# Causal attention stages of a decoder: probabilities made in their turned form from a second score product

## The chip, the cores and the metric

The program runs on one NeuronCore of a Trainium2 chip. The metric is the device time of one execution in microseconds, median of several. A core has five engines with queues of their own that meet only by semaphores: TensorE (PE: matmuls, and PEld: its weight loads), VectorE (DVE), ScalarE (ACT), GpSimd (POOL) and SyncE (SP, which issues DMAs).

## The reference, cut to what matters

Four decoder layers, each of three sub-blocks, on x of 16 items x 128 positions x 256 channels. Two of the sub-blocks hold causal self-attention over 16 heads of 16 channels: the first half of `_L1_ffn_ref` (layer norm ahead, no query, key or value bias) and `_L3_attn_ref` (with biases). Both are

```python
q = (x @ wq).reshape(b, t, HEADS, HEAD_DIM)          # keys and values likewise
scores = jnp.einsum('bqhd,bkhd->bhqk', q, k)
mask = jnp.arange(t)[:, None] < jnp.arange(t)[None, :]
scores = jnp.where(mask, -jnp.inf, scores)
attn = jax.nn.softmax(scores / np.sqrt(HEAD_DIM), axis=-1)
ctx = jnp.einsum('bhqk,bkhd->bqhd', attn, v).reshape(b, t, EMB)
return ctx @ wo + bo
```

## The kernel before, in words

The program is a row of stages, one for each sub-block, which keep x on the chip. `build` (L3823) makes them; `first_causal` (L3849) and `causal` (L3870) are `self_attention_stage` (L395) with `causal=True`. Each engine runs its part of a stage in the written order, and semaphore counts (`Count`, L34) tie them. A stage goes over 16 batch items. An item is split into two units (u = 0, 1; `NP` = 2) of eight heads, and the eight into two banks i of four heads k. In what follows n is a unit's number, 2b+u.

For one unit TensorE writes the causal mask into the two banks of `s_ps[u]` (two bf16 products with 512 columns, L643) and adds eight score products, queries in the rows (L650). A product has 32 contraction rows, so it occupies one of four row groups of the array: unit u uses groups 2u and 2u+1. There are two pairs of score banks, one for each unit of an item. VectorE takes the negated row maximum over all eight heads (L879). ScalarE makes `probs` by eight exponentials with the maximum as bias, each with a sum (L798). VectorE inverts the sums (L919), GpSimd multiplies (L569), TensorE turns the scaled probabilities by four transposes per bank (L664), ScalarE copies bank 0 and VectorE bank 1 to `pT` (L806, L886), and TensorE multiplies by the values (L690: four column groups of 32, one head pair in each). VectorE copies the context to `aT` (L912), TensorE multiplies by `wo` (L701), VectorE adds the residual (L926, or L929 with norm and moments).

Projections for the next item are laid between: queries and keys (L612, L620) in units u = 0, values (L629) in u = 1. `bank_d` is shared by keys, values and the output product, so that the value projection waits for the residual addition. ScalarE takes the queries from PSUM (L771, or L775 with biases), VectorE the keys and values (L893 to L906). GpSimd fetches x for item b+2 (L516, with norm L519 to L526), and adds the output bias (L549).

On TensorE the order of a unit is written out by hand in `unit` (L708): half of the transposes of the previous unit, projections, the weighing of the unit before that, the other half, the next unit's scores, the output product. Middle items run in a loop (`every_item`, L474).

A stage's beginning: GpSimd makes the constants (L500) and fetches two items; TensorE waits for weights and constants (L746) and turns item 0 (L605). The second stage begins inside the experts' stage ahead of it (`begun=True`): that stage issues its weight loads (L2361) between its own gathers, calls its constants and its fetches on GpSimd (L2443, L2450), and `take_first` and `take_second` on ScalarE (L2611).

Of the kernel before, what the change touches and what calls it, by code (L numbers as in the profile page):

```python
# [15 lines left out]
ALU = mybir.AluOpType  # L16
ACT = mybir.ActivationFunctionType
AX = mybir.AxisListType
F32 = mybir.dt.float32
BF16 = mybir.dt.bfloat16  # L20
# [3 lines left out]
P = 128  # L24
B = 16
# [83 lines left out]
def chunked(w, rows=P):  # L109

    return w.rearrange("(c p) n -> p c n", p=rows)


def row_everywhere(v, parts=P):

    return v.rearrange("(o n) -> o n", o=1).broadcast_to([parts, v.shape[0]])
# [272 lines left out]
def half_scales():  # L389

    low = (np.arange(P) // HEAD_DIM) % 2 == 0
    return (np.stack([low, ~low], axis=1) * np.float32(HEAD_DIM ** -0.5)).astype(np.float32)


def self_attention_stage(core, halves, wq, wk, wv, wo, out_bias, qkv_bias=None, causal=False, alibi=False,  # L395
# [10 lines left out]
    with ExitStack() as ctx:  # L406
# [595 lines left out]
        if context is not None:  # L1002
            c_used.advance(B)
            for n in c_landed:
                n.advance(16 * B)
        stage = Stage(sync, gpsimd, tensor, scalar, vector, out_used, x_saved if norm else out_used)
        stage.start = Start(load_weights, constants, fetch_two, take_first, take_second, biases, tables)
# [2815 lines left out]
def build(nc, a, out):  # L3823
    with ExitStack() as ctx:
# [18 lines left out]
        with ExitStack() as moe:  # L3843
# [4 lines left out]
            core.side = "right"  # L3848
            first_causal = self_attention_stage(core, a["half_scales"], a["L1_ffn_wq"], a["L1_ffn_wk"], a["L1_ffn_wv"],  # L3849
                                                a["L1_ffn_wo"], a["L1_ffn_bo"], causal=True, target=x1, norm=False,  # L3850
                                                pre_norm=(a["L1_ffn_ln1_scale"], a["L1_ffn_ln1_shift"]), after=over_context)
            core.side = "left"
# [16 lines left out]
        core.side = "left"  # L3869
        causal = self_attention_stage(core, a["half_scales"], a["L3_attn_Wq"], a["L3_attn_Wk"], a["L3_attn_Wv"],  # L3870
                                      a["L3_attn_Wo"], a["L3_attn_bo"], causal=True,
                                      qkv_bias=(a["L3_attn_bq"], a["L3_attn_bk"], a["L3_attn_bv"]), after=experts_b, begun=True)
        experts_b.leads_to(causal)
# [40 lines left out]
def laid_out(inputs):  # L3914
# [22 lines left out]
    a["head_rows"] = wide_head_rows()  # L3937
    a["half_scales"] = half_scales()
    a["mask_cols"] = a["mask_BxS2_fk1"].T
    a["lens_cols"] = a.pop("mask_BxS2_if0").T  # L3940
# [27 lines left out]
```

## Time and profile before

| | us |
|---|---|
| median of 3 runs (lowest, highest) | 3044.0 (3043.15, 3044.74) |
| profiled execution | 3048.76 |
| its span, first to last instruction | 3047.0 |

| engine | busy share of the span |
|---|---|
| PE, PEld | 88%, 73% |
| DVE | 53% |
| ACT | 46% |
| POOL | 46% |

The mean granted TensorE clock is 0.94 of full speed. Times of rows are us from the span's start. A busy PE means that some matmul is in flight; matmuls overlap, and a row's duration holds the last one's own flight. In a row that stands for several instructions (x4) the duration runs from the first start to the last end. The first causal stage lies at about 1124 to 1330, the second at about 2544 to 2742.

### The profile page before, as it was taken

How to read it: one execution, taken by the hardware profiler on the slowest of the kernel's cores; microseconds unless marked ns; L12 is line 12 of the kernel's file. 1: busy time of each engine (PE TensorE's matmuls, PEld its weight loads, DVE VectorE, ACT ScalarE, POOL GpSimd, SP SyncE). 2: the span in 40 equal slices, each digit the busy share in tenths (PEclk: the TensorE clock that was granted, in tenths of full speed). 3: DMA queues.
4: the chain of work that ended last, by engine and by line, in shares of the span. 5: the costliest groups of instructions: out<-in, count | busy, mean ns of one | idle time of the engine just before them, and what ended most of it. 6: DMA issues, size and time to landing. Idle time of an engine off the chain costs nothing.

```text
span 3047.0 us, 73166 instructions
## 1 busy us (share of the span) xinstructions
PE 2693.3 (88%) x26131; PEld 2215.5 (73%) x26189; DVE 1605.5 (53%) x3526; ACT 1412.8 (46%) x4543; POOL 1409.6 (46%) x1645
## 2 busy tenths in 40 slices
PE   7888897569989978978995889999996996999999
PEld 6777776447666656758994767878775995768888
DVE  7999999654456645561126763333333004556643
ACT  4666665434456647742226862223322335763210
POOL 3777777723356655543335662323232223663320
PEclk9999999769999989979997989999996998999999
DMA  3000000100000000027752020000005551010100
GB/s 100 2 2 2 2 2 2 56 30 1 24 15 14 17 20 1 0 84 237 240 195 77 0 95 8 11 10 7 10 19 178 180 171 53 0 49 29 53 10 20
DMA packets 96096, 154.49 MB, mean 51 GB/s; under 512 B 12256, under 2 KB 55904, under 8 KB 95600
## 3 DMA queue, kind: packets, MB, share of 16 engines
q1 hardware_dynamic: 89904, 134.92, 13.5%
q0 software_dynamic: 5952, 16.26, 1.5%
q8 instruction: 163, 2.67, 0.4%
q14 instruction: 77, 0.63, 0.1%
HBM read 136.74 MB, written 14.42 MB: 50 GB/s over the span
## 4 chain that ended last, share of the span: by engine, by line
PE 55%; POOL 4%; DVE 4%; issue 3%; ACT 3%; DMA 1%; SPq 0%; DVEq 0%; ACTq 0%; POOLq 0%
PE up_ps L2485 7%; PE e_out_ps L2503 5%; PE t_ps L664 4%; PE s_ps L650 3%; PE bank_a L1554 3%; PE bank_b L1554 3%; POOL probs L569 2%; PE bank_a L612 2%; PE bank_d L701 2%; ACT probs L798 2%; PE frame_ps L1633 2%; PE bank_d L620 2%; PE bank_b L1570 2%; PE bank_a L1570 2%; PE o_ps L690 2%
## 5 line engine op out<-in xcount | busy, mean ns | idle before, releaser
L569 POOL TENSOR_TENSOR probs<-probs,inv 128x512 f32<-128x512 f32 x320 | 327.9, 1039 | 277.8 <-DVE inv L919 277.5
L3437 POOL TENSOR_TENSOR hc<-h,bc 128x1024 f32<-128x1024 f32 x128 | 301.9, 2359 | 111.9 <-DVE h L3718 85.8
L798 ACT ACTIVATE probs<-s_ps,negmax 128x128 f32<-128x128 f32 (+1 forms) x768 | 297.1, 414 | 7.5 <-DVE negmax L879 6.0
L3718 DVE TENSOR_TENSOR_SCAN h<-da,dbu_ps 128x1024 f32<-128x1024 f32 x128 | 292.5, 2285 | 11.2 <-DVE dbu_ps L3730 4.6
L664 PE MATMUL t_ps<-ident,probs 128*128 128x128 f32 x1280 | 210.6, 288 | 57.7 <-POOL probs L569 49.5
L2485 PE MATMUL up_ps<-xT,w_lift 128*128 128x128 f32 x1984 | 234.3, 277 | 0.0
L664 PEld LDWEIGHTS t_ps<-ident,probs 128*128 128x128 f32 x1280 | 140.7, 142 | 124.9 <-POOL probs L569 58.4
L2485 PEld LDWEIGHTS up_ps<-xT,w_lift 128*128 128x128 f32 x1984 | 229.4, 194 | 0.1
L3665 ACT ACTIVATE da<-dta_ps 128x1016 f32<-128x1016 f32 x128 | 130.3, 1018 | 148.6 <-PE dta_ps L3527 148.3
L3527 PE MATMUL dta_ps<-dt,a_spread 32*128 32x128 f32 x2048 | 151.9, 287 | 44.6 <-ACT da L3665 20.8
L879 DVE TENSOR_REDUCE negmax<-s_ps 128x4 f32<-128x1024 f32 (+1 forms) x128 | 156.6, 1223 | 46.5 <-PE s_ps L650 44.5
L3527 PEld LDWEIGHTS dta_ps<-dt,a_spread 32*128 32x128 f32 x2048 | 127.5, 190 | 68.4 <-ACT da L3665 30.5
L806 ACT ACTIVATE pT<-t_ps 128x512 f32<-128x512 f32 x160 | 95.6, 597 | 164.7 <-PE t_ps L664 163.3
L2410 POOL DMA_INDIRECT rows<-expert_rows_in,row_from x62 | 60.3, 973 | 233.7 <-PE x_ps L2478 216.6
L798 ACT ACTIVATION_READ_ACCUMULATOR probs<-s_ps,negmax 128x1 f32 x768 | 168.3, 219 | 0.0
L3730 DVE TENSOR_TENSOR dbu_ps<-dbu_ps,bc 128x1024 f32<-128x1024 f32 x128 | 154.9, 1210 | 11.6 <-PE dbu_ps L3532 11.5
L2503 PE MATMUL e_out_ps<-w_down,hT 128*128 x680 | 156.7, 380 | 0.0
L3532 PE MATMUL dbu_ps<-dtu,spread 32*128 32x128 f32 x2048 | 152.0, 288 | 1.2 <-DVE h L3718 1.2
L1708 ACT ACTIVATE probs<-s_ps,negmax 128x128 f32<-128x128 f32 x256 | 89.9, 377 | 111.5 <-DVE negmax L1774 111.5
L2503 PEld LDWEIGHTS e_out_ps<-w_down,hT 128*128 128x128 f32 x680 | 124.8, 191 | 14.3
L650 PE MATMUL s_ps<-kT,q_low 32*128 32x128 f32 (+1 forms) x1024 | 130.6, 331 | 0.0
L3532 PEld LDWEIGHTS dbu_ps<-dtu,spread 32*128 32x128 f32 x2048 | 127.0, 190 | 1.5 <-DVE h L3718 1.5
(503 smaller groups left out, 6552.5 us busy)
## 6 DMA issues: line engine op xcount, KB each, us to landing
w_lift<-in_L_ffn_w SPq DMA_DIRECT2D x78, 512.0 KB, 4.7
w_lift<-in_L_ffn_w SPq DMA_DIRECT2D x23, 1024.0 KB, 5.0
cT<-in_ctx_turned SPq DMA_DIRECT2D x32, 256.0 KB, 2.6
w_down<-in_L_ffn_w SPq DMA_DIRECT2D x8, 1024.0 KB, 9.4
gathered<-expert_rows_out SPq DMA_DIRECT2D x12, 512.0 KB, 6.5
c_in<-in_ctx SPq DMA_DIRECT2D x16, 256.0 KB, 2.8
w_down<-in_L_ffn_w SPq DMA_DIRECT2D x8, 512.0 KB, 5.9
wkv<-in_L_xattn_Wkv SPq DMA_DIRECT2D x2, 2048.0 KB, 13.0
```

What stands on the lines that cost most here:

```text
L569: pool.tensor_tensor(probs[:, u % 2, i], probs[:, u % 2, i], inv[:, u % 2, HB * i:HB * (i + 1)].unsqueeze(2).broadcast_to([P, HB, W]), ALU ...
L650: last = pe.matmul(s_bank[:, i, k * W:(k + 1) * W], q[s][row:row + ROWS, j, qc, :], kT[row:row + ROWS, j, qc, :], start=not causal, stop=True,
L664: last = pe.transpose(t_ps[:, k * kt + t, :], probs[:, u % 2, i, k, t * P:(t + 1) * P], core.ident[:, :])
L798: last = act.activation(probs[:, u % 2, i, k, :], src, ACT.Exp, bias=negmax[:, u % 2, at], accum_out=sums[:, u % 2, at])
L879: dve.tensor_reduce(negmax[:, u % 2, :], scores, AX.X, ALU.max, negate=True).then_inc(negmax_done.sem, 1)
L1554: last = pe.matmul(bank[:, m, :], w[:, cc, col:col + P], src[:, cc, :], start=(cc == 0), stop=(cc == chunks_in - 1))
L2485: last = pe.matmul(up_ps[:, bank, m, :], lift_sb[:, i % LIFTS, k, cc, at:at + P], xT[:, i % 2, cc, :], start=(cc == 0), stop=(cc == DC - 1))
L2503: last = pe.matmul(out_ps[i % 2][:, 0:D], hT[:, i % 2, m, :], down_sb[:, e, m, :], start=(m == 0), stop=(m == HC - 1))
L3437: pool.tensor_tensor(hc[:, s % 4], h[:, s % 2], bc[:, j, 1, :].unsqueeze(1).broadcast_to([P, 2 * G, P]), ALU.mult).then_inc(hc_ready.sem, 1)
L3527: last_a = pe.matmul(dta_ps[:, i, g, :], a_spread[row:row + ROWS, s // 2, g, :], dt[row:row + ROWS, j, s // 2, :], start=True, stop=True)
L3532: last_u = pe.matmul(dbu_ps[si % 2][:, i, g, :], spread_sb[row:row + ROWS, g, :], dtu[row:row + ROWS, ji, si // 2, :], start=True, stop=True)
L3718: dve.tensor_tensor_scan(flat(h[:, s % 2]), flat(da[:, s % 4]), dbu_ps[s % 2][:, :, :, :].rearrange("p i g t -> p (i g t)"), 0.0, ALU.mult ...
```

## The change

Both causal stages move to a new function, `turned_attention_stage`. Scores are computed twice: queries in the rows, for the maximum alone, and keys in the rows, into `t_ps`, from which the exponential gives `pT` directly. For the second form the maximum must be subtracted per column: VectorE splits the negated maximum into three bf16 terms (`row_max`), TensorE turns the terms (`turn_max`), ScalarE copies them (`take_max`), and for each head a small product with a 0/1 matrix (`lower`) puts the sum of the terms into the bank ahead of the turned score. The mask is written ahead of the plain scores only; GpSimd zeroes later keys in `pT` (`leave_later_keys`). Sums come from products with ones (`counted`) beside the values, and VectorE divides the context (`take_context`). There is one pair of score banks and one pair of turned banks. The loops are written out. Constants grow from three to eight, and there is one more small weight load (`max_heads`).

```diff
+            def leave_later_keys(n):
+                pool.wait_ge(exp_done.sem, exp_done.done(n))
+                flat = pT[:, n % 2].rearrange("p i k t -> p (i k) t")
+                pool.affine_select(out=flat, in_=flat, compare_op=ALU.is_ge, fill=0.0, base=0,
+                                   pattern=[[0, 8], [1, P]], channel_multiplier=-1).then_inc(causal_done.sem, 1)
...
+            pool.wait_ge(loads.sem, weights)
+            pool.tensor_copy(which_max[:, :, :], heads_sb[:, :].unsqueeze(2).broadcast_to([P, 4, P])
+                             ).then_inc(consts.sem, 1)
...
+            def project_v(b):
+                pe.wait_ge(k_ready.sem, k_ready.done(b))
+                pe.wait_ge(out_used.sem, out_used.done(b - 2))
...
+            def leave_out(n):
+                pe.wait_ge(negmax_done.sem, negmax_done.done(n - 1))
...
+            def lower(n, i, k):
+                row = ROWS * (2 * (n % 2) + i)
+                pe.matmul(t_ps[:, i, k, :], which_max[row:row + ROWS, k, :], negmax_T[row:row + ROWS, :],
+                          start=True, stop=False, skip_group_check=True)
+
+            def score_both(n):
+                if n >= 0:
+                    pe.wait_ge(max_ready.sem, max_ready.done(n))
+                    pe.wait_ge(exp_done.sem, exp_done.done(n - 1))
+                    for k in range(4):
+                        for i in range(2):
+                            lower(n, i, k)
+                if n + 1 < UNITS and (n + 1) % 2 == 0:
+                    pe.wait_ge(q_ready.sem, q_ready.done((n + 1) // 2))
+                    pe.wait_ge(k_ready.sem, k_ready.done((n + 1) // 2))
+                for k in range(4):
+                    for i in range(2 if n + 1 < UNITS else 0):
+                        plain_last = score(n + 1, i, k)
+                    for i in range(2 if n >= 0 else 0):
+                        turned_last = score_turned(n, i, k)
...
+            def turn_max(n):
+                pe.wait_ge(negmax_done.sem, negmax_done.done(n))
+                pe.wait_ge(max_ready.sem, max_ready.done(n - 1))
+                pe.matmul(m_ps[:, 0, :], max_terms, core.ident_bf[:, :], start=True, stop=True
+                          ).then_inc(max_turned.sem, 1)
+
+            def weigh(n):
...
+                pe.wait_ge(causal_done.sem, causal_done.done(n))
+                pe.wait_ge(a_ready.sem, a_ready.done(n - 1))
...
+                for part in range(2):
+                    for i in range(2):
+                        for k in range(4):
+                            left = counted[:, i, :] if part else v[:, j, 4 * u + k, i * ROWS:(i + 1) * ROWS]
+                            last = pe.matmul(od_ps[k * ROWS:(k + 1) * ROWS, part, u, :], left, pT[:, n % 2, i, k, :],
+                                             start=(i == 0), stop=(i == 1), skip_group_check=True)
...
+            pe.wait_ge(loads.sem, weights)
+            pe.wait_ge(consts.sem, consts.done(7))
+            turn(0)
...
+            for n in range(UNITS):
+                b, u = n // 2, n % 2
+                score_both(n)
+                if n >= 1:
+                    weigh(n - 1)
+                if u == 0 and b + 1 < B:
+                    project_q(b + 1)
+                if u == 1 and b >= 1:
+                    out(b - 1)
+                if u == 1 and b + 2 < B:
+                    turn(b + 2)
+                if n + 1 < UNITS:
+                    turn_max(n + 1)
+                if n + 2 < UNITS:
+                    leave_out(n + 2)
+                if b + 1 < B:
+                    (project_v if u else project_k)(b + 1)
...
+            def exponentiate(n):
+                act.wait_ge(t_scored.sem, t_scored.done(n))
+                act.wait_ge(weighed.sem, weighed.done(n - 2))
+                act.activation(pT[:, n % 2].rearrange("p i k t -> p (i k t)"), t_ps[:, :, :, :].rearrange(
+                    "p i k t -> p (i k t)"), ACT.Exp).then_inc(exp_done.sem, 1)
...
+            for n in range(UNITS):
+                b, u = n // 2, n % 2
+                exponentiate(n)
+                if u == 0 and b + 1 < B:
+                    take_q(act, b + 1)
+                if u == 1 and b + 2 < B:
+                    copy_turned(act, b + 2)
+                if n + 1 < UNITS:
+                    take_max(n + 1)
...
+            def row_max(n):
+                u = n % 2
+                dve.wait_ge(scored.sem, scored.done(n))
+                dve.wait_ge(max_turned.sem, max_turned.done(n - 2))
+                dve.tensor_reduce(term(0, u), s_ps[:, :, :, :], AX.X, ALU.max, negate=True).then_inc(split.sem, 1)
+                dve.wait_ge(split.sem, split.done(2 * n))
+                dve.tensor_tensor(term(1, u), term(0, u), term_top(0, u), ALU.subtract).then_inc(split.sem, 1)
+                dve.wait_ge(split.sem, split.done(2 * n + 1))
+                dve.tensor_tensor(term(2, u), term(1, u), term_top(1, u), ALU.subtract).then_inc(negmax_done.sem, 1)
...
+            def take_context(n):
+                b, u = n // 2, n % 2
+                dve.wait_ge(weighed.sem, weighed.done(n))
+                dve.wait_ge(a_ready.sem, a_ready.done(n - 2))
+                dve.reciprocal(inv[:, u, :], od_ps[:, 1, u, :]).then_inc(inv_ready.sem, 1)
+                dve.wait_ge(inv_ready.sem, inv_ready.done(n))
+                dve.wait_ge(out_ready.sem, out_ready.done(b - 2))
+                dve.tensor_tensor(aT[:, b % 2, u, :], od_ps[:, 0, u, :], inv[:, u, :], ALU.mult).then_inc(a_ready.sem, 1)
...
+            for n in range(UNITS):
+                b, u = n // 2, n % 2
+                if n + 1 < UNITS:
+                    row_max(n + 1)
+                if n >= 1:
+                    take_context(n - 1)
+                if u == 0:
+                    if b + 2 < B:
+                        pre_moments(b + 2)
+                    if b + 1 < B:
+                        take_k(b + 1)
+                else:
+                    if b >= 1:
+                        finish(b - 1)
+                    if b + 1 < B:
+                        take_v(b + 1)
```

## Rows read from the trace of the kernel before

**Rows 1.** Busy us (instructions) by engine, then clock, DMA share, GB/s: first stage
```profile
1136.00:1330.00 194.00, 174.72 (x1712) 133.14 (x1739) 101.19 (x234) 131.90 (x604) 105.48 (x135) 0.96 0.00 1
```

**Rows 2.** Chain of waits, both stages: start, us, engine, tile, line
```profile
1211.79 0.89 PE bank_a L612 x8
...
1305.18 0.89 PE bank_a L612 x8
...
2594.29 1.09 PE s_ps L650 x16
...
2706.62 1.09 PE s_ps L650 x16
```

**Rows 3.** Timeline, first stage: start, us, engine, line, operation [idle before <-releaser]
```profile
1215.10 0.49 PE L650 MATMUL s_ps<-kT,q_low 32*128 32x128 f32 x4
...
1216.41 1.23 DVE L879 TENSOR_REDUCE negmax<-s_ps 128x8 f32<-128x1024 f32 x1 [0.78 <-PE s_ps L650]
...
1217.55 0.42 DVE L926 TENSOR_TENSOR x<-bank_d,xres 128x256 f32 x1
...
1218.03 1.13 PE L629 MATMUL bank_d<-wv,xT 128*128 128x256 f32 x4 [0.28 <-DVE x L926]
1218.54 0.18 DVE L858 BATCH_NORM_AGGREGATE pre_mv<-pre_stats 128x2 f32<-128x6 f32 x1 [0.15 <-DVE pre_stats L855]
...
1219.09 0.65 PE L690 MATMUL o_ps<-pT,v 128*32 128x128 f32 x16
...
1222.77 0.66 PE L664 MATMUL t_ps<-ident,probs 128*128 128x128 f32 x4 [0.55 <-POOL probs L569]
```

**Rows 4.** Timeline of another stage: products on four row groups, first and last of 16 rows
```profile
303.52 0.38 PE L3527 MATMUL dta_ps<-dt,a_spread 32*128 32x128 f32 x2
...
304.42 0.28 PE L3532 MATMUL dbu_ps<-dtu,spread 32*128 32x128 f32 x2
```

**Rows 5.** Timeline of the masked stage, which has ones products and divides its context
```profile
2800.03 0.65 PE L1194 MATMUL o_ps<-pT,v 128*32 128x128 f32 x16
2800.49 0.62 PE L1194 MATMUL o_ps<-pT,ones 128*32 128x128 f32 x16
...
2802.27 1.75 DVE L1299 RECIPROCAL inv<-o_ps 128x256 f32<-128x256 f32 x1
2804.05 0.42 DVE L1302 TENSOR_TENSOR aT<-o_ps,inv 128x256 f32<-128x256 f32 x1
```

**Rows 6.** Groups (count, busy us, mean ns, idle before), and one row of the timeline
```profile
L569 POOL TENSOR_TENSOR probs<-probs,inv 128x512 f32<-128x512 f32 x320 | 327.9, 1039 | 277.8 <-DVE inv L919 277.5
L3665 ACT ACTIVATE da<-dta_ps 128x1016 f32<-128x1016 f32 x128 | 130.3, 1018 | 148.6 <-PE dta_ps L3527 148.3
...
2628.42 0.86 ACT L775 ACTIVATE q_high<-bank_a,bq_half,half 128x128 f32<-128x128 f32 x2
```

**Rows 7.** Timeline of both stages' starts
```profile
1128.89 0.66 PE L605 MATMUL bank_a<-ident,x_in 128*128 128x128 f32 x2 [8.47 <-POOL x_in L526]
1129.55 1.22 POOL L526 TENSOR_SCALAR x_in<-x,pre_mv,pre_rstd 128x256 f32<-128x256 f32 x1
...
2538.38 0.43 SPq L488 DMA_DIRECT2D bv<-in_L_attn_bv  x1
...
2544.22 0.89 POOL L516 COPY x_in<-x 128x256 f32<-128x256 f32 x2 [0.75 <-ACT x L2601]
...
2551.08 0.36 ACT L759 ACTIVATE xT<-bank_a 128x256 f32<-128x256 f32 x1
...
2553.91 0.20 POOL L2441 TENSOR_TENSOR shift<-shift,rstd 128x4 f32<-128x4 f32 x1
```

**Rows 8.** Chain and timeline of the second stage's end
```profile
2723.39 1.11 PE s_ps L650 x16
...
2726.83 0.49 PE L650 MATMUL s_ps<-kT,q_low 32*128 32x128 f32 x4
...
2739.93 0.42 DVE L929 TENSOR_TENSOR y<-bank_d,xres 128x256 f32<-128x256 f32 x1 [1.22 <-PE bank_d L701]
```

## What the change should do, worked out before it was run

> **What bounds the kernel now.** I read first the stretch of a whole stage, to see that no engine is full and that the clock is granted. In the first causal stage TensorE has matmuls in flight for 174.72 of 194 us, ScalarE works 131.90, VectorE 101.19, GpSimd 105.48, at a granted clock of 0.96 [rows 1]; in-flight time is not work, so the next view matters more. The chain of waits shows the period of one batch item (two units of eight heads): in the first stage 1211.79 to 1305.18 for eight items, 11.67 us each; in the second stage 2594.29 to 2706.62 for ten, 11.23 us each [rows 2]. Almost every link of it is TensorE. Then the order of one unit: a score block of eight products starts at 1215.10, VectorE's maximum starts at 1216.41, the residual addition ends at 1217.97 and lets the value projection start at 1218.03 after 0.28 us of waiting, and in the first stage the next transposes wait 0.55 us for GpSimd's scaling [rows 3]. So TensorE sets the pace, with about 1 us of waits per item in the first stage and 0.3 in the second; the rest is its own issue time.
>
> **TensorE's sum hardly changes.** Per unit the change removes eight transposes of the probabilities; four show 0.66 with the last one's own 0.27 in it [rows 3], so about 0.43 of issue, 0.86 for eight. It adds eight turned score products, eight products with ones, eight small bf16 products that lower the scores by the maximum, and one bf16 transpose of the maxima. The turned scores come in the two row groups that the plain ones leave free. Another stage of this kernel already interleaves products on all four row groups: 32 matmul instructions (16 products) from 303.52 to the last start at 304.42 [rows 4], against a whole block of 1.09 us for eight products here [rows 2]. Hence sixteen cost what eight cost, 0.9 us plus a change of array shape, together 1.09: the second score product is free. The ones products are in the trace too: 16 instructions each for values and ones, from 2800.03 to a last end at 2801.11, less a matmul's own 0.27 some 0.83 us of issue, where the values alone take 0.43 [rows 5]: +0.4 us. The lowering products have no row: at least 0.21 us (an estimate, a quarter of the 0.88 that eight f32 products take), at most twice that; I take 0.3, between them, as pairs on two row groups are nearest to the score rows. The transpose of the maxima: 0.16 with its exposed weight load (estimate). Sum: -0.86 + 0 + 0.4 + 0.3 + 0.16 = 0.0 us per unit, and one change of array shape less (about 0.2 us each: the block's 1.09 less its 0.9 of issue).
>
> A rule speaks against the free product. The 32 matmuls of [rows 4], each with its own load of 128 columns, fit into 0.99 us, 31 ns a load. The Trainium skill, "TensorE: Matmul & The Clock Gate", section "LDWEIGHTS (loading the stationary operand)", says that a load takes its columns divided by 1.2 in ns whatever the rows; by that, an estimate from the page, 32 loads are 3.4 us a unit and the change would cost some 150 us more. The trace has four row groups at the faster pace, so it decides.
>
> **The new loop is a VectorE chain.** There is one score bank pair now, not two, and behind the scores of a unit VectorE does in order: maximum, two small subtractions, the reciprocal and product of the previous unit's context, then the addition or copy for which TensorE waits. I lay a unit out from S, the first score product.
> Sixteen products end at S+1.18 (303.52 to 304.42 plus 0.28) [rows 4], the maximum starts 0.15 later at S+1.33 and takes 1.23: S+2.56 [rows 3]. Two splits, each a wait on itself of 0.15 and a small operation of 0.18 as in the aggregate's row [rows 3]: S+3.22. Bounds: 0.15 each if they follow without the wait, 0.4 each at worst. The reciprocal now covers 128 columns of PSUM instead of 4: the row for 256 columns is 1.75 us, so 0.88 to 1.0; I take 0.92, and 0.03 + 0.29 for the multiplication (256 columns take 0.42, starting 0.03 after the reciprocal) [rows 5]: S+4.46.
> A rule on the size: 1.75 us for 256 columns is 6.8 ns a column. The Trainium skill, "VectorE: DVE Perf Modes", section "First, the fixed hardware budget", says that a reciprocal is an iterative divide with a repeat count of 8; with the page's 0.96 GHz that would be an estimated 1.07 us for 128 columns, and some 6 us more on the whole. By the row it is less.
> In odd units the residual addition follows (0.42 plus its start, S+4.90), the value projection can start at S+4.95, where TensorE, free since about S+3.9, has stood still; value projection and change of shape are 1.06 (1218.03 to 1219.09) [rows 3], the lowering 0.3: next S after 6.32 us.
> In even units of the first stage come the moments (0.43 + 0.15 + 0.18) and the key copy (0.42), S+5.66, so the next S is after 5.72. In even units of the second stage ScalarE ends last: the query projection ends about S+3.3 (1.09, weighing 0.83, shape 0.2, projection 0.89, 0.29 handing over), four scalings take 1.54 (two pairs, the second of 0.86) [rows 6], copying the transposed maxima 0.38 (the pairs give 0.43 each, the long row a floor of 0.13), then the lowering: S after 5.57.
> So an item takes 12.04 us in the first stage (+0.37) and 11.89 in the second (+0.66). Over the 14.5 steady items: +5.4 and +9.6, together +15.0.
>
> **Off the path.** GpSimd loses two scalings of 1.04 us for 512 elements and gains one selection of 1024; 1.1 to 2.1 us by that row [rows 6], and the weighing comes a whole unit after the exponential, so I price it at nothing; if it took over about 5 us it would show. ScalarE's eight short exponentials with sum reads become one of 1024 columns, 1.02 us [rows 6]. That was beside TensorE's work before, and gives nothing.
>
> **The starts cost.** TensorE's first transpose now waits for all eight constants, the last of which (which_max) GpSimd makes only after both items are fetched. First stage: the second x_in ends at 1130.77; with four more small constants (0.7 at 0.2 or less each, as the row at 2553.91 shows) and a 512-wide copy (0.8; two of 256 take 0.89) the transpose starts near 1132.3 instead of 1128.89: +3.4 [rows 7]. Second stage: the experts' scaling on GpSimd ends at 2554.11, the tenth weight load pushes the gathers and with them this by 0.5, then the copy 0.8 and a transpose 0.66: ScalarE's copy of xT starts about 2556.2 instead of 2551.08, +5.1 [rows 7]. Sum +8.5.
>
> **The ends** nearly cancel. A first and a last unit without projections took 3.44 us (2723.39 to 2726.83) and last now about 4.4 (S+3.22, transposing 0.5, copying 0.4, lowering 0.3): +0.4 to +1.0 each, four times, about +3.2. From the last scores to the last addition it was 13.10 us [rows 8]; now S+4.1 for the maximum's way, turned scores 1.0, exponential 1.1, selection 1.2, weighing 1.2, context 1.4, output 1.3, about 11.5: -1.6 twice. Total: 15.0 + 8.5 + 0 = +23.5, rounded to +24. The profiled execution spans 3047.0 (3048.76 with what lies around it, 4.8 over the median of 3044.0); the same +24 on the median gives 3068 us.
>
> **Rivals.** (a) TensorE's own work sets the pace: if VectorE's chain ended under TensorE's 3.9 us after S in each unit, an item would be twice 2.6 (0.3, 0.88, 0.83, 0.16, 0.43), four projections of 0.88, a turn of 0.2 and six shape changes, 10.1 us: -1.6 and -1.1 over 14.5 items is -39, less the starts' 8.5, so 3013 us, faster. For it: TensorE's sum is equal, and two waits go. Against: the chain to S+4.46 is made of rows. 0.08. (b) The reciprocal at a copy's pace, 0.29: odd units 5.69, even ones 5.54 and 5.57, items -0.45 and +0.03, so 3046 us, no change. Against it stands the 1.75 row. 0.07. (c) Sixteen products on four row groups at the pace of pairs, 0.88 more in each of 62 units: +55 on top, 3123 us, slower. It decides if the new order or the loads hold the four groups apart; [rows 4] speak against. The page's rule on loads is the far end of the same case. 0.07. (d) Waits that I don't see, between that and the forecast, 0.04. (e) The forecast, slower by 24 us, through VectorE's chain and the late constant: 0.74; its own range by the bounds (lowering 0.21 to 0.43, splits, copy, starts) is 3056 to 3084.
>
> **Numbers.** Slower by more than 0.2%, about what a measurement can tell (6 us): most of (e), (c) and (d), 0.83. Within: half of (b) and the low edge of (e), 0.07. Faster: (a) and a little of (b), 0.10. The range 3044 to 3090 leaves out (a), (c) and a part of (d).
>
> **What would show it.** Items 12.0 and 11.9 us apart. In odd units TensorE's wait ahead of the value projection at some 1.1 us, released by VectorE's residual addition, and before even units' scores a wait for the key copy (first stage) or ScalarE's copied maxima (second). Sixteen score products within 1.2 us. Reciprocal rows near 0.92 us. First transposes near 1132 and ScalarE's first xT copy near 2556. I am wrong if the value projection starts without a wait, if the score block is nearer 2 us, or if the stages' starts stay put.

## The result and the profile after

The changed kernel takes 3096.9 us (median of 4 runs, 3093.06 to 3100.88) against 3043.6 for the kernel before beside it: ratio 1.0173, 95% interval 1.0161 to 1.0184. It is slower by 53 us. The forecast was +24 us (3044 to 3090): the engine and the stages were right, the size less than half. The sign came out right through a cause that the forecast didn't have, which was luck: without that cause the same kernel measures no change (below).

The page of the changed kernel: the busy shares, and the share of each engine in the chain that ended last.

```profile
PE 2695.1 (87%) x28301; PEld 2217.3 (72%) x28301; DVE 1688.7 (54%) x3526; ACT 1278.5 (41%) x3583; POOL 1350.8 (44%) x1591
...
PE 52%; DVE 10%; issue 4%; ACT 3%; POOL 3%; DMA 1%; SPq 0%; ACTq 0%; DVEq 0%; POOLq 0%
```

ScalarE's share is 5 points lower, the others are within 2. What has moved is who stands in the chain of the causal stages. Before, no operation of VectorE had a large share in it: in the second stage it was almost TensorE alone [rows 2], in the first it also ran through GpSimd (more on that below). Now, of the stretch from 1160 to 1320, the chain is made of the following (by engine, tile and line, share of the stretch; then pieces by start and us):

```profile
by line: DVE negmax L1407 19.3%; DVE negmax L1409 16.7%; PE s_ps L1235 12.4%; PE bank_d L1209 8.3%; PE bank_d L1200 7.3%; DVE inv L1438 7.2%; DVE negmax L1411 5.7%; issue 5.6%; PE s_ps L1224 3.5%; DVE kT L1418 3.4%; PE t_ps L1239 3.3%; DVE 
...
1230.36 1.24 DVE negmax L1407
...
1236.76 1.24 DVE negmax L1407
...
1243.23 1.24 DVE negmax L1407
```

L1407 is the maximum, L1409 and L1411 are the two split operations, L1438 the reciprocal. The maximum recurs at 1230.36 and 1243.23: 12.87 us an item where it was 11.67 [rows 2] and 12.04 was forecast. In the second stage it is 12.23 (maxima at 2670.28 and 2682.51), where it was 11.23 and 11.89 was forecast. L1409, an operation on eight elements a partition, holds 16.7% of the chain. The timeline of one odd unit of the changed kernel shows it (start, us, engine, line, operation; what ended the idle time before):

```profile
1229.16 0.38 PE L1235 MATMUL s_ps<-kT,q_low 32*128 32x128 f32 x2 [0.28 <-DVE kT L1418]
...
1230.06 0.28 PE L1239 MATMUL t_ps<-q_high,kT 32*128 32x128 f32 x2
...
1230.36 1.23 DVE L1407 TENSOR_REDUCE negmax<-s_ps 128x8 f32<-128x1024 f32 x1 [1.35 <-PE s_ps L1235]
1230.41 1.02 ACT L1363 ACTIVATE pT<-t_ps 128x1024 f32<-128x1024 f32 x1 [2.88 <-PE t_ps L1239]
...
1231.51 1.09 POOL L1162 TENSOR_SCALAR_AFFINE_SELECT pT<-pT 128x1024 f32<-128x1024 f32 x1 [0.52 <-ACT pT L1363]
1231.62 1.00 DVE L1409 TENSOR_TENSOR negmax<-negmax 128x8 f32<-128x8 f32 x1
...
1232.65 0.17 DVE L1411 TENSOR_TENSOR negmax<-negmax 128x8 f32<-128x8 f32 x1
...
1232.74 0.95 DVE L1438 RECIPROCAL inv<-od_ps 128x128 f32<-128x128 f32 x1
...
1234.49 1.10 PE L1209 MATMUL bank_d<-wv,xT 128*128 128x256 f32 x4 [0.95 <-DVE x L1449]
...
1235.55 0.38 PE L1235 MATMUL s_ps<-kT,q_low 32*128 32x128 f32 x2
```

Sixteen score products run within 1.18 us (1229.16 to 1230.34). The exponential ends at 1231.43, GpSimd's selection follows from 1231.51 to 1232.60, and the first split, which starts 0.11 later, ends at 1232.62, with it. The second split, of the same shape, takes 0.17. In even units the second one meets another operation of GpSimd. Three timelines of the changed kernel, the last from the second stage:

```profile
1225.14 1.09 POOL L1162 TENSOR_SCALAR_AFFINE_SELECT pT<-pT 128x1024 f32<-128x1024 f32 x1 [5.41 <-ACT pT L1363]
1225.15 1.10 DVE L1409 TENSOR_TENSOR negmax<-negmax 128x8 f32<-128x8 f32 x1
...
1226.19 0.72 POOL L1141 TENSOR_TENSOR xres<-x,out_bias 128x256 f32<-128x256 f32 x1
1226.28 0.66 DVE L1411 TENSOR_TENSOR negmax<-negmax 128x8 f32<-128x8 f32 x1
...
2671.53 1.13 POOL L1162 TENSOR_SCALAR_AFFINE_SELECT pT<-pT 128x1024 f32<-128x1024 f32 x1 [3.29 <-ACT pT L1363]
2671.53 0.17 DVE L1409 TENSOR_TENSOR negmax<-negmax 128x8 f32<-128x8 f32 x1
2671.74 0.95 DVE L1411 TENSOR_TENSOR negmax<-negmax 128x8 f32<-128x8 f32 x1
```

At 2671.53 both start together: now the first split takes 0.17 and the second 0.95, to the selection's end. Where the two engines meet, VectorE's small operation ends when GpSimd's does. That is a theory until something is moved.

What TensorE waited for from 1160 to 1290 (us in total, times, longest):

```profile
PE m_ps L1269 <- DVE negmax L1411: 11.6, 20, 0.9
PE bank_d L1209 <- DVE x L1449: 9.5, 10, 1.0
PE s_ps L1235 <- DVE kT L1418: 2.8, 10, 0.3
```

The largest of these waits is for the second split, ahead of the transpose of the maxima (L1269). No such wait was forecast.

Accounting on the profiled runs: the first stage's moments (L3106 now, L2619 before) start 22.0 us later (1352.41 against 1330.40), the second stage's first copy of xT 32.3 later (2583.41 against 2551.08), and the first product behind the second stage 52.4 later (2792.84 against 2740.41). A second pair of profiled runs ("The stretch between", below) has 19.4, 28.7 and 46.6 at the same three places. So the first stage costs 19 to 22 with its start, the second 18 to 20, and 9 to 10 arise between.

### The profile page after: what moved, and what is told of

Its sections match the earlier page's. It is cut to its first block, busy times and chain, and to the rows that moved or that the text cites. A ratio compares the mean times of both kernels' runs of the same rounds, so it can differ in the third digit from the quotient of the medians.

```text
span 3099.1 us, 75292 instructions
## 1 busy us (share of the span) xinstructions
PE 2695.1 (87%) x28301; PEld 2217.3 (72%) x28301; DVE 1688.7 (54%) x3526; ACT 1278.5 (41%) x3583; POOL 1350.8 (44%) x1591
## 4 chain that ended last, share of the span: by engine, by line
PE 52%; DVE 10%; issue 4%; ACT 3%; POOL 3%; DMA 1%; SPq 0%; ACTq 0%; DVEq 0%; POOLq 0%
PE up_ps L2972 7%; PE e_out_ps L2990 5%; PE bank_a L2041 3%; PE bank_b L2041 3%; PE t_ps L664 2%; DVE negmax L1407 2%; PE frame_ps L2120 2%; PE bank_b L2057 2%; ACT probs L798 2%; PE bank_a L2057 2%; POOL probs L569 2%; PE s_ps L1235 2%; DVE negmax L1409 2%; PE s_ps L650 2%; PE gate_ps L276 1%
## 5 line engine op out<-in xcount | busy, mean ns | idle before, releaser
L4205 DVE TENSOR_TENSOR_SCAN h<-da,dbu_ps 128x1024 f32<-128x1024 f32 x128 | 292.5, 2285 | 11.3 <-DVE dbu_ps L4217 4.4
L569 POOL TENSOR_TENSOR probs<-probs,inv 128x512 f32<-128x512 f32 x192 | 196.7, 1040 | 164.1 <-DVE inv L919 164.0
L1162 POOL TENSOR_SCALAR_AFFINE_SELECT pT<-pT 128x1024 f32<-128x1024 f32 x64 | 70.4, 1100 | 239.0 <-ACT pT L1363 239.0
L664 PE MATMUL t_ps<-ident,probs 128*128 128x128 f32 x768 | 126.5, 288 | 41.4 <-POOL probs L569 34.3
L664 PEld LDWEIGHTS t_ps<-ident,probs 128*128 128x128 f32 x768 | 82.7, 142 | 87.2 <-POOL probs L569 41.5
L1363 ACT ACTIVATE pT<-t_ps 128x1024 f32<-128x1024 f32 x64 | 65.5, 1024 | 181.3 <-PE t_ps L1239 181.3
L798 ACT ACTIVATE probs<-s_ps,negmax 128x256 f32<-128x256 f32 x256 | 117.5, 476 | 3.1 <-DVE negmax L879 2.5
L1407 DVE TENSOR_REDUCE negmax<-s_ps 128x8 f32<-128x1024 f32 x64 | 78.4, 1225 | 69.8 <-PE s_ps L1235 69.8
L3234 DVE TENSOR_TENSOR hT<-up_ps,silu 128x512 f32<-128x512 f32 x39 | 27.0, 691 | 146.8 <-PE up_ps L2972 146.8
```

The lines of the kernel that those rows point to most:

```text
L569: pool.tensor_tensor(probs[:, u % 2, i], probs[:, u % 2, i], inv[:, u % 2, HB * i:HB * (i + 1)].unsqueeze(2).broadcast_to([P, HB, W]), ALU ...
L664: last = pe.transpose(t_ps[:, k * kt + t, :], probs[:, u % 2, i, k, t * P:(t + 1) * P], core.ident[:, :])
L798: last = act.activation(probs[:, u % 2, i, k, :], src, ACT.Exp, bias=negmax[:, u % 2, at], accum_out=sums[:, u % 2, at])
L1407: dve.tensor_reduce(term(0, u), s_ps[:, :, :, :], AX.X, ALU.max, negate=True).then_inc(split.sem, 1)
L4205: dve.tensor_tensor_scan(flat(h[:, s % 2]), flat(da[:, s % 4]), dbu_ps[s % 2][:, :, :, :].rearrange("p i g t -> p (i g t)"), 0.0, ALU.mult ...
```

## The experiments

Theory T1: a VectorE operation with both inputs in SBUF stands still while GpSimd works on SBUF. Rivals: T2, the splits are slow in themselves (their second operand is a bf16 half of each f32 word); T3, any use of SBUF by GpSimd does it; T4, the selection is simply late for the weighing.

**Selection later.**

```diff
             def leave_later_keys(n):
                 pool.wait_ge(exp_done.sem, exp_done.done(n))
+                if n + 1 < UNITS:
+                    pool.wait_ge(negmax_done.sem, negmax_done.done(n + 1))
```

> GpSimd's selection of unit n also waits until the maximum of unit n+1 is split, so it no longer runs beside the two split operations. Theory T1 (a VectorE operation with both inputs in SBUF stands still while GpSimd works on SBUF): the first split takes 0.18 instead of 1.05 us, the second 0.17, items come 12.0 us apart in the first stage and 11.9 in the second, and the total falls from 3097 by some 15 to 30 us, to 3067 to 3082. Rival T2 (the splits are slow in themselves, through their strided bf16 halves): the first split stays at 1.0 us and the total within 4 us of 3097. Rival T4 (the selection's end was what mattered, the weighing waits for it): slower than 3097, with a wait of the weighing for pT.

Measured: 3045.4 us (10 runs) against 3044.5 before, ratio 1.0004 (0.9994 to 1.0013), below the 3067 to 3082 that were expected. One wait, on an engine that is not on the path, gives back 51.5 of the 53 us. The timeline of this kernel, the same odd unit:

```profile
1216.42 0.38 PE L1237 MATMUL s_ps<-kT,q_low 32*128 32x128 f32 x2 [0.28 <-DVE kT L1420]
...
1217.62 1.23 DVE L1409 TENSOR_REDUCE negmax<-s_ps 128x8 f32<-128x1024 f32 x1 [1.34 <-PE s_ps L1237]
...
1218.88 0.17 DVE L1411 TENSOR_TENSOR negmax<-negmax 128x8 f32<-128x8 f32 x1
1219.08 0.17 DVE L1413 TENSOR_TENSOR negmax<-negmax 128x8 f32<-128x8 f32 x1
1219.17 0.95 DVE L1440 RECIPROCAL inv<-od_ps 128x128 f32<-128x128 f32 x1
1219.38 1.09 POOL L1164 TENSOR_SCALAR_AFFINE_SELECT pT<-pT 128x1024 f32<-128x1024 f32 x1 [1.48 <-DVE negmax L1413]
...
1220.15 0.29 DVE L1443 TENSOR_TENSOR aT<-od_ps,inv 128x128 f32<-128x128 f32 x1
1220.36 0.41 DVE L1451 TENSOR_TENSOR x<-bank_d,xres 128x256 f32<-128x256 f32 x1
...
1220.92 1.10 PE L1211 MATMUL bank_d<-wv,xT 128*128 128x256 f32 x4 [0.55 <-DVE x L1451]
1221.96 0.23 PE L1245 MATMUL t_ps<-negmax_T,which_max 32*128 32x128 bf16 x2
1221.98 0.38 PE L1237 MATMUL s_ps<-kT,q_low 32*128 32x128 f32 x2
...
1226.81 0.42 DVE L1420 COPY kT<-bank_d 128x256 f32<-128x256 f32 x1 [0.26 <-PE bank_d L1202]
...
1228.58 1.23 DVE L1409 TENSOR_REDUCE negmax<-s_ps 128x8 f32<-128x1024 f32 x1 [1.34 <-PE s_ps L1237]
```

Both splits take 0.17, here and in all 64 units: T2 falls, and so does T4, since the selection now ends later and the kernel is faster. The wait keeps the splits off the selection and, in even units, off the addition behind it (L1141), so what it gives back is the price of both meetings. The reciprocal (0.95), the product (0.29) and the residual addition (0.41) run beside the same selection at their usual durations; each reads PSUM and at most one tile in SBUF. Items are 10.96 us apart (1217.62 to 1228.58), less than the 12.0 that T1's expectation had taken from the forecast. So the theory of the cause holds, and my sum for a unit without it was too large by 1 us an item; more on that below.

**Half a selection.**

```diff
-                flat = pT[:, n % 2].rearrange("p i k t -> p (i k) t")
+                flat = pT[:, n % 2, 0]
...
-                                   pattern=[[0, 8], [1, P]], channel_multiplier=-1).then_inc(causal_done.sem, 1)
+                                   pattern=[[0, 4], [1, P]], channel_multiplier=-1).then_inc(causal_done.sem, 1)
```

> Leaves out part of the work: the selection covers four of the eight heads, the other four keep the probabilities of later keys. The selection's duration falls from 1.09 to about 0.57 us. T1: the first split lasts until the selection ends, so about 0.5 us instead of 1.05, and the total falls by 0.5 us in each of 62 units where it is on the path, 15 to 30 us, to about 3070 to 3080. T2: split still 1.0, total 3097.

Measured: 3066.9 us, ratio 1.0084 (1.0061 to 1.0106): 30 us back, 3 below the range that was expected. The timeline:

```profile
1209.63 0.64 POOL L1162 TENSOR_SCALAR_AFFINE_SELECT pT<-pT 128x512 f32<-128x512 f32 x1 [0.53 <-ACT pT L1363]
1209.74 0.55 DVE L1409 TENSOR_TENSOR negmax<-negmax 128x8 f32<-128x8 f32 x1
```

The selection ends at 1210.27, the split at 1210.29. An unchanged VectorE instruction follows the length of another engine's.

**A write instead of the selection.**

```diff
-                flat = pT[:, n % 2].rearrange("p i k t -> p (i k) t")
-                pool.affine_select(out=flat, in_=flat, compare_op=ALU.is_ge, fill=0.0, base=0,
-                                   pattern=[[0, 8], [1, P]], channel_multiplier=-1).then_inc(causal_done.sem, 1)
+                pool.wait_ge(causal_done.sem, causal_done.done(n - 1))
+                pool.memset(written[:, :], 0.0).then_inc(causal_done.sem, 1)
```

> Leaves out part of the work: in place of the selection, GpSimd sets a tile of the same size that nobody reads to zero (some 0.95 us by the 1.38 for 1536 columns), at the same moment; it writes SBUF but reads nothing, and later keys keep their probabilities. T1 in its narrow form (the two share a way to read): the first split takes 0.18 us and the total falls to 3067 to 3082. T3 (any use of SBUF by GpSimd holds VectorE off): the split lasts until that operation ends, 0.8 to 0.9 us, and the total falls by under 10 us. The Trainium skill, "SBUF — State Buffer", in its list of which operations contend, has a VectorE instruction with two SBUF inputs contend with a GpSimd instruction that reads SBUF and not with one that only writes; by it the first holds.

Measured: 3043.7 us, ratio 0.9999 (0.9989 to 1.0008), again below the 3067 to 3082 expected, since that range too came from the forecast's 12.0 us an item. The timeline:

```profile
1215.47 0.95 POOL L1163 MEMSET written<- 128x1024 f32 x1 [4.71 <-ACT pT L1363]
1215.49 0.17 DVE L1409 TENSOR_TENSOR negmax<-negmax 128x8 f32<-128x8 f32 x1
1215.69 0.17 DVE L1411 TENSOR_TENSOR negmax<-negmax 128x8 f32<-128x8 f32 x1
```

GpSimd works on SBUF in the same place and for nearly the same time, but reads nothing, and the splits take 0.17 beside it. T3 falls. The two GpSimd operations that held a split back, the selection and the addition L1141, read SBUF, and the one that didn't doesn't read: what they contend for is reading. (The memset also differs from the selection as an operation; none was tried that differs in the reading alone.) This is the rule of the Trainium skill, "SBUF — State Buffer", section "Who interferes with whom": a VectorE instruction with two SBUF inputs contends with a GpSimd instruction that reads SBUF, not with one that only writes. The traces agree in every point they can show: 1.00 to 1.10 beside the selection, 0.17 beside the memset, and at 2671.53, where the profile can't tell which started first, the split was let through. The total lands within 2 us of the later selection, so no other effect of the selection is larger than these measurements can tell (some 4 us).

**The late constant.** The fifth step of the forecast, by itself: TensorE's first transpose no longer waits for which_max.

```diff
-            pe.wait_ge(consts.sem, consts.done(7))
+            pe.wait_ge(consts.sem, consts.done(6))
...
                 if n >= 0:
+                    if n == 0:
+                        pe.wait_ge(consts.sem, consts.done(7))
```

> TensorE's first transpose waits for seven constants; the eighth, which_max, is waited for only ahead of the first lowering products. By the rows of the changed kernel the first query projection comes at about 1132.0 instead of 1134.9 (its x_in is there at 1130.3) and in the second stage at about 2579.3 instead of 2583.9 (ScalarE's scaling of the experts' rows ends at 2578.9 and is then last). Theory S1: total 7 us less, 3090 (the forecast had put the two starts at 8.5). Rival S2 (the starts were bound by the fetch and the experts' rows anyway): within 2 us of 3097.

Measured: 3090.5 us, ratio 1.0152 (1.0135 to 1.0169), 6.4 less than the changed kernel. The intervals of the two kernels overlap, so this total alone doesn't decide; the starts in the trace do, and so does the next pair of kernels, whose intervals are apart. S1 holds. In the second stage (first two lines the changed kernel, next two this one):

```profile
2581.76 0.61 POOL L1134 CAST which_max<-max_heads 128x512 bf16<-128x512 f32 x1
2582.58 0.66 PE L1185 MATMUL bank_a<-ident,x_in 128*128 128x128 f32 x2 [25.50 <-POOL which_max L1134]
```

```profile
2570.15 0.66 PE L1185 MATMUL bank_a<-ident,x_in 128*128 128x128 f32 x2 [14.98 <-POOL x_in L1112]
...
2576.45 0.36 ACT L1324 ACTIVATE xT<-bank_a 128x256 f32<-128x256 f32 x1
```

Counted from the first stage's moments, the transposes come 10 us sooner (1219.94 instead of 1230.17), the copy of xT only some 5 (1226.24 instead of 1231.00), since ScalarE's scaling of the experts' rows is then last, as in the kernel before [rows 7].

**Both.** The two edits together:

> The later selection and the earlier start together. If the two are independent, the total is 3045.4 less 6.4, 3039 us, 0.2% under the kernel before; if the earlier start had only been hidden in a stage that waits anyway, 3045.

Measured: 3036.2 us against 3045.4, ratio 0.9970 (0.9959 to 0.9982): 9.2 less where 6.4 was expected, additive within what the intervals can tell. The idea of the change, without its two accidents, is 0.3% faster than the kernel before.

**Residual first.** Does VectorE's order set the pace then?

```diff
+                if u == 1 and b >= 1:
+                    finish(b - 1)
                 if n >= 1:
                     take_context(n - 1)
```

and finish(b - 1) leaves its old place, behind take_context.

> As later_start, and in odd units VectorE does the residual addition ahead of the reciprocal and product. Theory V (VectorE's chain up to the residual addition sets the start of the value projection): TensorE's wait of 0.5 us per item in both stages goes (the output product ends at about S+3.2, S being the first score product, TensorE is free at S+4.0), items 10.45 instead of 10.96 us, 29 items: 3039 less 15 is 3024 us. Rival W (TensorE waits for the delivery of its own earlier products, the reciprocal is beside them): items stay at 10.96, 3039 us; it could be slower if the context product becomes late for the next weighing.

Measured: 3025.5 us, ratio 0.9935 (0.9922 to 0.9949), 10.7 less where 15 was expected. Items are 10.32 and 10.39 us apart in the two stages, down from 10.96 and 10.99 (10.45 was expected), so the items gave what was asked of them and the total less: stretches that no edit touches differ from kernel to kernel by as much (see below). Theory V holds: the value projection has no wait any more (timeline).

```profile
1208.42 0.17 DVE L1415 TENSOR_TENSOR negmax<-negmax 128x8 f32<-128x8 f32 x1
...
1209.04 0.42 DVE L1453 TENSOR_TENSOR x<-bank_d,xres 128x256 f32<-128x256 f32 x1 [0.46 <-PE bank_d L1219]
1209.38 0.95 DVE L1442 RECIPROCAL inv<-od_ps 128x128 f32<-128x128 f32 x1
1209.62 1.10 PE L1211 MATMUL bank_d<-wv,xT 128*128 128x256 f32 x4
```

**Keys first.** In even units project_k moves ahead of leave_out:

```diff
+                if u == 0 and b + 1 < B:
+                    project_k(b + 1)
                 if n + 2 < UNITS:
                     leave_out(n + 2)
-                if b + 1 < B:
-                    (project_v if u else project_k)(b + 1)
+                if u == 1 and b + 1 < B:
+                    project_v(b + 1)
```

> As residual_first, and in even units the key projection comes ahead of the mask product of 0.6 us, so that the copy of the keys lies beside that product. Theory: the wait of 0.28 us for the keys goes in the first stage's 15 items, while in the second stage ScalarE's four scalings end last and nothing changes: 3020 us, 4 less than residual_first. Rival: a change of array shape is added and takes it back: within 2 us of residual_first.

Measured: 3018.4 us, ratio 0.9908 (0.9893 to 0.9923), 7.1 less than residual first where 4 was expected. The times of the two kernels don't overlap (3017.7 to 3021.2 and 3023.0 to 3030.6), though their profiled executions are only 2 us apart. Items of the first stage went from 10.32 to 9.95 us, some 5 us in all; those of the second stayed at 10.39, as expected. Its rows:

```profile
1207.46 1.22 DVE L1413 TENSOR_REDUCE negmax<-s_ps 128x8 f32<-128x1024 f32 x1 [1.34 <-PE s_ps L1237]
...
1217.41 1.22 DVE L1413 TENSOR_REDUCE negmax<-s_ps 128x8 f32<-128x1024 f32 x1 [1.34 <-PE s_ps L1237]
```

That is 9.95 us an item in the first stage, where TensorE now waits for nothing in the records from 1160 to 1286. This is rival (a) of the prediction, TensorE's own work, which it had put at 10.1.

**Queries first.** In even units of the second stage project_q goes ahead of the weighing.

```diff
+                first = pre_norm is None and u == 0 and b + 1 < B
+                if first:
+                    project_q(b + 1)
                 if n >= 1:
                     weigh(n - 1)
-                if u == 0 and b + 1 < B:
+                if u == 0 and b + 1 < B and not first:
                     project_q(b + 1)
```

> As key_first, and in the even units of the second stage the query projection comes ahead of the weighing, so that ScalarE can scale the queries 1.1 us sooner. Theory: TensorE's wait of 0.5 us for the copied maxima, behind the four scalings, goes; items of the second stage 9.9 to 10.0 instead of 10.4 us, 14 of them, 7 us, total 3012. Rival: the weighing, now later, pushes VectorE's reciprocal and the copy of the keys, which is next late: under 3 us of gain, 3016 or more.

Measured: 3016.1 us, ratio 0.9919 (0.9904 to 0.9933). The wait for the copied maxima is all but gone (from 2580 to 2690 one of 0.4 us, where there were ten, 4.6 us together) and items of the second stage take 10.15 us instead of 10.40, half of what was expected: two more changes between kinds of product seem to take the rest, which is not separated. The two medians are 2 us apart and the ratios, each against the kernel before in its own comparison, overlap, so this edit's gain isn't shown in the total.

**The stretch between.** Both kernels again, unchanged:

> The kernel before, profiled again. In the profiled run of the changed kernel some 5 us of the difference arose between the two causal stages, in code that the change does not touch. If that is how one run differs from another, the stretch from the first stage's last residual addition to the second stage's start differs by several us here too; if it belongs to the change, the stretch repeats within 1 us of 1220.7 us (moments at 1330.40, first copy of xT at 2551.08).

> The changed kernel, profiled again, for the same question: if the 5 us belong to the change, the stretch from 1352.41 to 2583.41 repeats within 1 us of 1231.0 us; if they are how one run differs from another, it comes out several us shorter or longer.

Measured: before 1220.9 us (1330.79 to 2551.67), after 1230.2 us (1350.19 to 2580.40). The difference repeats, so it isn't how one run differs from another. The late constant is 4 to 5 of it (1226.2 and 1226.5 in the two kernels that only start earlier or start earlier and select later). The rest, some 5 us, arises in code that the change doesn't touch: counted from the stretch's start, VectorE's operations in the changed kernel are late by 0.9 to 1.1 us at 57 us, by 2.8 at 610 and by 5.2 at 1012, in both of its profiles. It is no fixed price of the change: with the same code in that stretch, residual first, keys first and queries first measured 1221.1, 1224.6 and 1220.3.

What goes along with it is the granted clock. Read from the profile in steps of 8 us, TensorE stood at the lower of its two levels (1.2 instead of 2.4 GHz) for 200 us of this stretch in both profiles of the kernel before, for 218 and 214 in those of the changed kernel, 206 and 210 with the earlier start, and 193, 211 and 203 in the last three kernels. In the first 60 us of the stretch the mean granted clock was 0.57 before and 0.54 after. Which of the two came first, a later instruction or less clock, no run separates; the cause stays open. The stretch behind the second stage, which no edit touches either, took 305.3 to 311.1 us in the twelve profiles. A few us of any total here can come from such stretches.

## Why the prediction was wrong in size, by its own steps

**Bound now: right for the second stage, in part for the first.** "Almost every link of it is TensorE" is so in the second stage. In the first, the chain of the kernel before leaves TensorE once an item, for 5.4 of 11.67 us (pieces of the chain by start and us, 1217.40 to 1222.77):

```profile
1217.96 0.44 DVE pre_stats L855
...
1219.80 1.22 POOL x_in L526
...
1221.71 1.01 POOL probs L569
...
1222.77 0.66 PE t_ps L664 x4
```

TensorE had work of its own beside that and stood still for only 0.28 and 0.55 us of it, so the forecast's 1 us of waits an item is right.

**TensorE's work: the second product is free, and the sum was a little too high.** Sixteen score products on four row groups took 1.18 us, where the block of eight took 1.09, so rival (c), at 3123 us, is out. Values and ones took 1.01 (1230.26 to 1231.27). The keys-first kernel, at 9.95 us an item without a wait, confirms the 10.1 that rival (a) had added up. It isn't equal work, as the sum of 0.0 had it: without its waits (0.9 and 0.3 us an item) the kernel before took 10.7 and 11.0. The Trainium skill's rule on loads ("TensorE: Matmul & The Clock Gate", section "LDWEIGHTS (loading the stationary operand)"), added up load by load, was to make the change 150 us dearer. These loads can't be added up: they overlap, 32 of them within the 1.18 us.

**VectorE's chain: the right mechanism, in the right place.** The value projection waits for the residual addition 0.95 us in each odd unit (1.1 forecast). But the chain was wrong in two terms of opposite sign. Us after the first score product S of an odd unit, from the rows above:

| | forecast | changed kernel | selection later |
|---|---|---|---|
| maximum starts | 1.33 | 1.20 | 1.20 |
| second split ends | 3.22 | 3.66 | 2.83 |
| value projection starts | 4.95 | 5.33 | 4.50 |
| next first score product | 6.32 | 6.39 | 5.56 |

The step that failed is "two splits 0.15+0.18 each". Its price came from the row of the aggregate [rows 3], which has one input, and its bounds were 0.15 to 0.4 each. The first split measured 1.05 on the mean, the second 0.41 (16 each, 1217 to 1320):

```profile
L1409 DVE TENSOR_TENSOR negmax<-negmax 128x8 f32<-128x8 f32 x16 | 16.8, 1053 | 0.5
...
L1411 DVE TENSOR_TENSOR negmax<-negmax 128x8 f32<-128x8 f32 x16 | 6.6, 414 | 0.6
```

Tied to it is the step on GpSimd: "I price it at nothing" looked only at when the selection's result is needed, a unit later, and not at what it holds while it runs. A selection starts the moment the exponential ends, and the exponential and the maximum are released by the same block of products and take 1.02 and 1.23 us: so from the second unit on it meets one split or both in every unit. Both operands of the split and the selection's input stand in the diff; the meeting could be read off before. Its price over both stages, with the addition L1141 that holds back the second split in even units, is the 51.5 us that the one wait gives back.

**The other error ran the other way.** Without the meeting an item takes 10.96 us in the first stage and 10.99 in the second, where 12.04 and 11.89 were forecast. In an odd unit 0.39 us were too many on VectorE's way to the end of the splits (two operations follow each other every 0.20, without the 0.15 of waiting that I added to each, and the maximum starts 0.13 sooner), and 0.3 were too many for the lowering: its products start at 1221.96 and the score products at 1221.98, beside them, not behind them. Even units took 5.40 instead of 5.72, and there VectorE's chain was no longer what ended last: its copy of the keys waited 0.26 us for TensorE's key projection (1226.81), so the forecast's path through the moments was off the path. Over 14.5 items this made steady work 28.7 us too dear: 14.5 times 1.08 and 0.90. With these terms right the forecast would have been about 3039 us, faster than before, and would have missed the meeting by its whole price. So two errors of opposite sign partly cancelled, and "slower" was right by luck: the kernel without the meeting measures 3045.4 us against 3044.5.

**Reciprocal: right.** 0.94 to 0.95 for 128 columns (0.92 forecast from [rows 5]), so rival (b) is out. The estimate of 1.07 from the Trainium skill ("VectorE: DVE Perf Modes", section "First, the fixed hardware budget") is 0.12 too high.

**Starts: right mechanism, about the right size.** +8.5 forecast, 6.4 measured by the run that removes the wait from the changed kernel, 9 by the one that removes it beside the later selection. The sign "first transposes near 1132" can't be judged by the clock of the trace: in two profiles of the changed kernel they come at 1133.25 and 1131.02, in two of the kernel before at 1128.89 and 1131.24. Counted from the first constant (L1097, before L501) it is 7.8 against 5.0 in both pairs, +2.8 where 3.4 was forecast.

**Ends and the rest: too low.** The forecast's ends nearly cancelled, with a slip: its seven terms for the way out of a stage add up to 11.3, not 11.5. Less the steady items (14.5 times 1.20 and 1.00), the first stage took 0 to 2 us more than before and the second 3 to 6. The cause of this stays open. And about 5 us in the untouched stages have no step in the forecast.

**Numbers.** Slower had 0.83 and it came so. The range ended at 3090 because the only cause that could lift the time beyond it, in my list, was a TensorE one (c), and "waits that I don't see" had 0.04. That share was too small for a new VectorE chain, in which every delay counts at once.

## What to carry to other kernels

When a chain moves to VectorE, write beside each of its operations where its inputs lie, and beside each operation of GpSimd when it starts and whether it reads SBUF: a two-input operation of 0.17 us becomes one of 1.1 if the two meet, and a wait on the engine that has time to spare can be worth more than the change itself (51 us here). Price a new dependence twice, once for when its result is needed and once for what the engine holds meanwhile. And put first in an engine's queue what another engine waits for; here that, with the rest, turned 1.7% slower into 0.9% faster. And when the sign of a forecast comes true, ask whether its own mechanism gave the sign: here it hadn't.

## What the runs showed of the hardware beyond that

It isn't always VectorE that is held: at 2671.53, with equal starts, the split took 0.17, and the selection 1.13 instead of the 1.09 that it takes in the odd units there; the next ones like it, at 2683.76 and 2695.99, are the same. Operations of VectorE that read PSUM, or one tile in SBUF, kept their duration beside a GpSimd that reads (0.95, 0.29 and 0.41 beside the selection at 1219.38). And the small bf16 products that lower the scores didn't hold up the plain f32 score products issued behind them: 0.02 us lie between the first starts of the two kinds (1221.96 and 1221.98), which use different row groups and write different banks of PSUM. The turned score products, in the same two row groups as the lowering ones, start at 1222.19. The records of one load of 32x128 f32 last 0.19 us on the mean, and 32 of them fit into 1.0 us on four row groups.
